# Projections of a transformer block in fp32 parts: the first slice of Wc loaded ahead of x, the first block's transposes in four banks, products begun tile by tile, the other blocks' transposes in two halves

## The chip, the cores and the metric

The kernel runs on one core of one Trainium2 chip, as one program written instruction by instruction for each engine: TensorE (matmuls, transposes), VectorE, ScalarE, GpSimd, and SyncE, which issues most of the loads and stores. The metric is the device time of an execution in microseconds, from which less is better. An engine works its own queue in order; engines wait for one another by semaphores that count up.

## The reference

The kernel computes one transformer layer with conditioning (adaptive layer norm) on x of 2 x 2048 x 512 in float32, with H = 512, 16 heads of 32 and an inner width of 2048:

```python
c6 = jax.nn.silu(c) @ Wc + bc
sh_msa, sc_msa, g_msa, sh_mlp, sc_mlp, g_mlp = jnp.split(c6, 6, axis=-1)
xm = _modulate(_ln(x), sh_msa, sc_msa)          # ln(x) * (1 + scale) + shift
q, k, v = xm @ Wq + bq, xm @ Wk + bk, xm @ Wv + bv
w = softmax((q / DH) k^T) per head
x = x + g_msa * ((w v) @ Wo + bo)
xm2 = _modulate(_ln(x), sh_mlp, sc_mlp)
x = x + g_mlp * (gelu(xm2 @ W1 + b1) @ W2 + b2)
```

c is the condition, 2 x 512; Wc is 512 x 3072, so that c6 has six slices of 512 for each of the two batches.

## The kernel before

The program has three stages one behind the other: `project` (0 to some 350 us of the profile), `attend`, and `feed_forward`. The diff touches only `project`.

**Tiling.** The 4096 tokens are 8 blocks of 512 (`NBLK`, index k, blocks 0 to 3 are batch 0). A block is normalised (`norm`, VectorE; its square root is `root` on GpSimd), transposed by TensorE in four tiles t of 128 features (`transposes`, L604, four 128x128 transposes a tile), scaled and shifted by ScalarE from PSUM into xm (`modulate`, L529, two buffers), and split by VectorE into a high part, rounded to the fp32r format, and a low part, the rest (`split_xm`: the cast L411 and the subtraction L413). Each product is the sum of three matmuls per tile, high by high, high by low, low by high (`three`, L610 to L612), twelve in all. A block has 12 products of this kind (`PER_BLOCK`): m = 0 to 7 are q and k in turn for the four groups of heads, m = 8 to 11 are v for four groups of tokens. They go round four PSUM banks (`mm_bank`). ScalarE takes each result (`take_qk`, L540, L543; L557 for v), VectorE splits those of q and k (`split_qk`, L420, L422), SyncE stores them.

**Order in a block.** The norm of block k + 1 stands at the start of VectorE's part of block k. TensorE transposes block k + 1 after product 3 of block k, ScalarE modulates after taking product 3, VectorE splits xm after splitting product 3. The transposes use two banks (`t_bank`) in turn, and so tile t waits until tile t - 2 has been modulated (the semaphore t_taken, which starts at 2).

**Early maxima.** From block 4 on, TensorE also runs score matmuls for the attention's row maxima (`early`, L644), two behind each of products 4 to 11 (in block 7 other counts), into `c_bank` and `g_bank` in turn. VectorE reduces each (L483). Matmul n waits until the reduce of n - 2 is done, as it uses the same bank. On VectorE the reduces for product m - 1 stand ahead of the `split_qk` of product m (`behind`).

**Start.** SyncE issues six small loads of biases and the condition, then x of block 0 (L273), two slices of Wc (L275), the weights Wq, Wk, Wv and x of block 1, each of 1 MB. TensorE forms silu(c) @ Wc for a slice (`part_rows`, L581), ScalarE copies it (`take_rows`, L522), TensorE turns it to columns (`part_columns`, L590), VectorE adds the bias and, for a scale, 1.0 (`mod_columns`, L441, L445). The first two slices (shift and scale of the attention) are needed for the first `modulate`; the second `part_columns` waits for the first `mod_columns` (g_taken). VectorE's queue there is norm(0), mod_columns(0), high_w(0), mod_columns(1), split_xm(0), and then high and low parts of Wk and Wv. The low part of Wq is GpSimd's (L364). TensorE waits for all four tiles of xm to be split, `pe.wait_ge(xm_split, 2 + KT * (k + 1))`, ahead of the first product of a block, and in each product for its weight's low part, `pe.wait_ge(w_split[m % 2 if m < N_QK else 2], 1)`.

Of the kernel before, what the change touches and what calls it, by code (L numbers as in the profile page):

```python
# [4 lines left out]
F32 = mybir.dt.float32  # L5
# [6 lines left out]
P = 128  # L12
# [162 lines left out]
def project(nc, sh, late, x, c, Wc, bc, Wq, bq, Wk, bk, Wv, bv, b1, bo, b2):  # L175
# [5 lines left out]
    with ExitStack() as ctx:  # L181
# [40 lines left out]

        rows_in, w_in, wide_in = sem("rows_in"), [sem(f"w_in{n}") for n in range(3)], sem("wide_in")
# [8 lines left out]
        w_hi_ready, w_split = sem("w_hi_ready"), [sem(f"w_split{n}") for n in range(3)]  # L232
# [13 lines left out]
        PARTS = (0, 1, 3, 4, 2, 5)  # L246
        RESULTS = (0, 1, 2, 3, 4, 6, 8)
# [4 lines left out]
        LAST_RESULT = 8  # L252

# [15 lines left out]
        def _(sp):  # L269
# [3 lines left out]
            sp.dma_start(xb[0][:, :, :], x_blocks[0]).then_inc(x_in[0], 16)  # L273
# [3 lines left out]
            load_wc(0)  # L277
            load_wc(1)
# [99 lines left out]
        def _(v):  # L378
# [27 lines left out]
            def split_xm(k, q):  # L406

                v.wait_ge(mm_done, PER_BLOCK * (k - 1) + 1) if not isinstance(k, int) or k > 1 else None
                for t in range(KT):
# [18 lines left out]
            v.tensor_scalar(sh.bq_scaled[:, :], sh.vecs[:, ROW_BQ:ROW_BQ + KT], 1.0 / DH, None, ALU.mult).then_inc(vecs_ready, 1)  # L428
            v.wait_ge(const_ready, 5)
# [6 lines left out]
            def mod_columns(e, column, one):  # L436
# [6 lines left out]
                if one:  # L443
                    after(last)
                    last = v.tensor_scalar(sh.mod[:, :, column:column + KT], sh.mod[:, :, column:column + KT], 1.0, None, ALU.add)  # L445
# [10 lines left out]
            def result(e, b):  # L456
                if e == 2:
                    mod_columns(e, SHIFT_MLP, False)
                elif e == 3:
                    mod_columns(e, SCALE_MLP, True)  # L460
                else:
                    gate(e, b)
# [5 lines left out]
            mod_columns(0, SHIFT_MSA, False)  # L468
            high_w(0).then_inc(w_hi_ready, 1)
            mod_columns(1, SCALE_MSA, True)  # L470
            split_xm(0, 0)
            for n in (1, 2):
                after(high_w(n))
                v.tensor_tensor(w_lo[:, n, :, :], w_raw[n], w_hi[:, n, :, :].bitcast(F32), ALU.subtract).then_inc(w_split[n], 1)
# [20 lines left out]
            def body(k, i, q, has_next):  # L495
                if has_next:
                    norm(k + 1, i + q, 1 - q)
                for m in range(N_QK // 2):
                    behind(k, m)
                if has_next:  # L500
                    split_xm(k + 1, 1 - q)
                for m in range(N_QK // 2, N_QK):
                    behind(k, m)
# [1232 lines left out]
```

## Time and profile before

| | |
|---|---|
| time of the kernel, median of 3 runs | 2750.54 us (2748.51 to 2750.82) |
| profiled execution, in all | 2751.63 us |
| its span, from first to last instruction | 2749.8 us |
| mean granted clock of TensorE | 0.995 |

The span is made of busy and idle time on five engines. For each instruction the timeline gives its start and duration; idle time ahead of it is written in brackets with what ended it (the releaser). "PEld" is TensorE loading weights, beside its matmuls. An engine's idle time costs nothing where another engine sets the pace. A matmul's duration contains its way through the array, which overlaps with the next: the distance between two starts is what it costs.

### The profile page before, as it was taken

What the parts mean: (1) busy time and instruction counts of PE and PEld (TensorE: products, weight loads), DVE (VectorE), ACT (ScalarE), POOL (GpSimd) and SP (SyncE); (2) the same over time, 40 slices, a digit from 0 to 9 for tenths busy, and PEclk for the clock granted to TensorE, in tenths of its full rate; (3) what the DMA queues carried; (4) which work ended last, traced back from release to release, by engine and by line L of the source; (5) the groups of instructions that cost most, each with busy time, mean ns of one, the idle gap of its engine ahead of it and who ended that gap; (6) DMA issues with size and microseconds to landing.
All of it is one profiled execution on the core that took longest, in us unless ns stands there. A gap on an engine that the chain in (4) does not pass through costs nothing. (4 is left out here: it accounts for less than half of the span.)

```text
span 2749.8 us, 37932 instructions
## 1 busy us (share of the span) xinstructions
PE 2702.7 (98%) x13737; PEld 1781.6 (65%) x13737; DVE 1999.2 (73%) x3323; ACT 1345.7 (49%) x2537; POOL 1867.9 (68%) x1080
## 2 busy tenths in 40 slices
PE   7999999999999999999999999999999999999998
PEld 5777755555555555555555555554688888888887
DVE  6456688788888888888888888776576765765754
ACT  2322266676676667767676776675221221221211
POOL 1000078989989999999989989896555555455553
PEclk9999999999999999999999999999999999999999
DMA  6555458788888879878888887875400100110000
GB/s 241 186 178 188 157 122 177 166 185 181 176 182 175 187 166 191 182 166 186 172 186 184 173 187 167 194 145 123 146 35 16 47 31 16 46 43 4 31 16 16
DMA packets 143754, 369.22 MB, mean 134 GB/s; under 512 B 23572, under 2 KB 40528, under 8 KB 119760
## 3 DMA queue, kind: packets, MB, share of 16 engines
q0 software_dynamic: 26784, 195.05, 35.5%
q1 hardware_dynamic: 96000, 155.26, 18.9%
q10 hardware_dynamic: 20784, 16.49, 2.0%
q8 instruction: 110, 1.80, 0.3%
q14 instruction: 76, 0.62, 0.1%
HBM read 111.97 MB, written 58.97 MB: 62 GB/s over the span
## 5 line engine op out<-in xcount | busy, mean ns | idle before, releaser
L1059 DVE TENSOR_REDUCE part_max<-shared_bank 128x1 f32<-128x512 f32 x1972 | 1206.8, 679 | 275.3 <-PE shared_bank L1179 275.3
L1034 ACT ACTIVATE probs<-s_bank 128x512 f32<-128x512 f32 x2048 | 1037.1, 629 | 291.7 <-PE s_bank L1195 287.6
L1206 PE MATMUL y_bank<-probs,vs 128*32 128x512 f32 x4096 | 496.2, 602 | 0.0
L881 POOL TENSOR_TENSOR first_sum<-probs 128x1024 f32<-128x1024 f32 x124 | 348.2, 2818 | 79.1 <-ACT probs L1034 77.0
L1622 ACT ACTIVATE h<-shared_bank,vecs 128x512 f32<-128x512 f32 x128 | 88.0, 687 | 564.0 <-PE shared_bank L1646 559.2
L1195 PE MATMUL s_bank<-late_parts 97*128 97x512 f32 x848 | 349.5, 414 | 1.0 <-ACT probs L1034 1.0
L881 POOL TENSOR_TENSOR half_sum<-probs 128x1024 f32<-128x1024 f32 x124 | 340.1, 2775 | 15.2 <-ACT probs L1034 14.9
L892 POOL TENSOR_TENSOR wo<-probs 128x1024 f32<-128x1024 f32 x124 | 338.5, 3115 | 0.4 <-ACT probs L1034 0.4
L1179 PE MATMUL shared_bank<-late_parts 96*128 96x512 f32 x848 | 336.8, 398 | 0.9
L892 POOL TENSOR_TENSOR second_sum<-probs 128x1024 f32<-128x1024 f32 x128 | 320.9, 2670 | 19.4 <-ACT probs L1034 10.2
L1432 POOL TENSOR_TENSOR late_parts<-w_raw,late_parts 128x512 fp32r<-128x512 f32 x96 | 129.1, 1345 | 227.7 <-DVE late_parts L1509 227.7
L1206 PEld LDWEIGHTS y_bank<-probs,vs 128*32 128x32 f32 x4096 | 107.2, 109 | 243.6 <-issue 125.0
L1195 PEld LDWEIGHTS s_bank<-late_parts 97*128 97x128 f32 x848 | 160.1, 189 | 133.4 <-issue 88.0
L1519 DVE CAST h_hi<-h 128x512 fp32r<-128x512 f32 x128 | 79.3, 619 | 179.9 <-ACT h L1622 179.8
L1644 PE MATMUL acc_bank<-w_hi,h_hi 128*128 128x512 f32 x512 | 201.5, 394 | 1.4 <-DVE h_lo L1521 1.2
L1644 PE MATMUL shared_bank<-late_parts 128*128 128x512 f32 x508 | 201.3, 396 | 1.1 <-PEq L740 1.1
L1646 PE MATMUL acc_bank<-w_hi,h_lo 128*128 128x512 f32 x512 | 200.8, 392 | 0.0
L1646 PE MATMUL shared_bank<-late_parts 128*128 128x512 f32 x508 | 199.4, 392 | 0.0
L1645 PE MATMUL acc_bank<-w_lo,h_hi 128*128 128x512 f32 x512 | 199.0, 389 | 0.0
L1645 PE MATMUL shared_bank<-space_parts,late_parts 128*128 128x512 f32 x508 | 198.8, 391 | 0.0
L1179 PEld LDWEIGHTS shared_bank<-late_parts 96*128 96x128 f32 x848 | 161.3, 190 | 30.5 <-DVE part_max L1059 5.4
L1195 PE MATMUL s_bank<-space_parts,late_parts 97*128 97x512 f32 x432 | 177.8, 412 | 0.0
(204 smaller groups left out, 4579.9 us busy)
## 6 DMA issues: line engine op xcount, KB each, us to landing
half_sum<-second_sum POOLq DMA_DIRECT2D x62, 1024.0 KB, 13.5
first_sum<-wo POOLq DMA_DIRECT2D x62, 1024.0 KB, 9.9
half_sum<-first_sum POOLq DMA_DIRECT2D x62, 1024.0 KB, 7.7
q_parts<-qk_out SPq DMA_DIRECT2D x32, 512.0 KB, 3.5
k_parts<-qk_out SPq DMA_DIRECT2D x32, 512.0 KB, 3.5
late_parts<-q_parts SPq DMA_DIRECT2D x63, 256.0 KB, 11.5
late_parts<-k_parts SPq DMA_DIRECT2D x60, 256.0 KB, 11.9
late_plain<-in_x SPq DMA_DIRECT2D x12, 1024.0 KB, 7.5
```

The costliest lines, as they stand in the source:

```text
L881: pool.tensor_tensor(first_home(c)[:, hs, :], probs[:, 4 * c % RING, hs, :], probs[:, (4 * c + 1) % RING, hs, :], ALU.add).then_inc(first_ ...
L892: pool.tensor_tensor(second_home(c)[:, hs, :], probs[:, (4 * c + 2) % RING, hs, :], probs[:, (4 * c + 3) % RING, hs, :], ALU.add).then_inc ...
L1034: act.activation(probs[:, tile % RING, h, :], s_bank[(HPG * tile + h) % 3][:, :], ACT.Exp).then_inc(p_done, 1)
L1059: v.tensor_reduce(part_max[:, i % 2, hs, c:c + 1], m_bank[ring.bank["max", i, n]][:, :], AX.X, ALU.max).then_inc(m_taken, 1)
L1179: pe.matmul(m_bank[ring.bank["max", i, n]][:, :], queries[i % 3][0:STACK, h, s * P:(s + 1) * P], keys[u][0:STACK, h, :], start=True, stop= ...
L1195: pe.matmul(s_bank[n % 3][:, :], keys[u][0:STACK + 1, h, s * P:(s + 1) * P], queries[i % 3][0:STACK + 1, h, :], start=True, stop=True).the ...
L1206: last = pe.matmul(y_bank[h * DH:(h + 1) * DH, :], vs[:, t, h * DH:(h + 1) * DH], probs[:, tile % RING, h, :], start=(t == 0), stop=(t == ...
L1432: pool.tensor_tensor(feed.w1_lo(j), w1_raw[j * 4 // MT][:, :, j % (MT // 4) * P:(j % (MT // 4) + 1) * P], feed.w1_hi(j).bitcast(F32), ALU. ...
L1622: act.activation(h[:, j % 2, :], up_bank[j % 2][:, :], ACT.Gelu, bias=sh.vecs[:, ROW_B1 + j:ROW_B1 + j + 1]).then_inc(up_taken, 1)
L1644: pe.matmul(bank, hi_l, hi_r, start=first, stop=False)
L1645: pe.matmul(bank, hi_l, lo_r, start=False, stop=False)
L1646: return pe.matmul(bank, lo_l, hi_r, start=False, stop=last)
```

## The change

- SyncE issues Wc's first slice ahead of x of block 0.
- The 1.0 of the two scales is added once to the bias columns in `vecs`, at the start, and no longer in `mod_columns`.
- Block 0's transposes of tiles 2 and 3 go to `mm_bank[2]` and `mm_bank[3]` (`x_bank`), so that they wait for no `modulate`.
- The first product of each block waits for xm tile by tile, inside `three`, in place of the wait for all four ahead of it.
- The high part of Wk is made by ScalarE (after its modulate of block 0), and VectorE's subtraction for Wk waits for it (wk_hi_ready).
- For blocks 1 to 7 transposes, modulate and split of xm are done in two halves (`HALF_AT`): tiles 0 and 1 behind product 3 as before, tiles 2 and 3 behind product 4, on each of the three engines.

```diff
--- before.py
+++ after.py
@@ -220,6 +220,9 @@
         g_bank = pb("g_bank", [P, H])
         m_bank = [c_bank, g_bank]
 
+        def x_bank(k, t):
+            return mm_bank[t] if k == 0 and t >= 2 else t_bank[t % 2]
+
         rows_in, w_in, wide_in = sem("rows_in"), [sem(f"w_in{n}") for n in range(3)], sem("wide_in")
         wc_in = [sem(f"wc_in{n}") for n in range(6)]
         x_in = [sem(f"x_in{n}") for n in range(2)]
@@ -229,7 +232,7 @@
         em_done, em_taken, early_neg = sem("em_done"), sem("em_taken"), sem("early_neg")
         silu_ready, select_ready = sem("silu_ready"), sem("select_ready")
         c_done, c_taken, g_done, g_taken = sem("c_done"), sem("c_taken"), sem("g_done"), sem("g_taken")
-        w_hi_ready, w_split = sem("w_hi_ready"), [sem(f"w_split{n}") for n in range(3)]
+        w_hi_ready, wk_hi_ready, w_split = sem("w_hi_ready"), sem("wk_hi_ready"), [sem(f"w_split{n}") for n in range(3)]
         stats_ready, rstd_ready, xn_ready = sem("stats_ready"), sem("rstd_ready"), sem("xn_ready")
         t_done, t_taken, xm_split = sem("t_done"), sem("t_taken"), sem("xm_split")
         mm_done, mm_taken, qk_split = sem("mm_done"), sem("mm_taken"), sem("qk_split")
@@ -244,12 +247,16 @@
         PER_BLOCK = 2 * G + TT
         N_QK = 2 * G
         PARTS = (0, 1, 3, 4, 2, 5)
+        SCALE_PARTS = (1, 4)
         RESULTS = (0, 1, 2, 3, 4, 6, 8)
 
 
         ROWS_AT = {(1, 0): 2, (1, 4): 3, (2, 0): 4, (3, 0): 5}
         RESULT_AT = {(1, 2): (2, 0), (1, 6): (3, 0), (2, 2): (4, 0), (2, 5): (4, 1), (3, 2): (5, 0), (3, 5): (5, 1)}
         LAST_RESULT = 8
+
+
+        HALF_AT = {N_QK // 2 - 1: (0, 1), N_QK // 2: (2, 3)}
 
 
 
@@ -270,11 +277,12 @@
             for r, v, n in ((ROW_BC, bc, 6 * KT), (ROW_BQ, bq, KT), (ROW_BK, bk, KT), (ROW_BV, bv, KT), (ROW_B1, b1, MT)):
                 sp.dma_start(rows[r:r + n, :], v.rearrange("(r p) -> r p", p=P)).then_inc(rows_in, 16)
             sp.dma_start(rows[ROW_C:ROWS, :], c.rearrange("b (t p) -> (b t) p", p=P)).then_inc(rows_in, 16)
-            sp.dma_start(xb[0][:, :, :], x_blocks[0]).then_inc(x_in[0], 16)
+
             def load_wc(e):
                 sp.dma_start(wc[e % 2][:, :, :], wc_parts[PARTS[e]]).then_inc(wc_in[e], 16)
 
             load_wc(0)
+            sp.dma_start(xb[0][:, :, :], x_blocks[0]).then_inc(x_in[0], 16)
             load_wc(1)
             for n, w in enumerate((Wq, Wk, Wv)):
                 sp.dma_start(w_raw[n], w.rearrange("(t p) n -> p t n", p=P)).then_inc(w_in[n], 16)
@@ -403,10 +411,11 @@
                                            ALU.subtract, ALU.mult)
                 last.then_inc(xn_ready, 1)
 
-            def split_xm(k, q):
-
-                v.wait_ge(mm_done, PER_BLOCK * (k - 1) + 1) if not isinstance(k, int) or k > 1 else None
-                for t in range(KT):
+            def split_xm(k, q, ts):
+
+                if k > 1:
+                    v.wait_ge(mm_done, PER_BLOCK * (k - 1) + 1)
+                for t in ts:
                     v.wait_ge(t_taken, 2 + KT * k + t + 1)
                     v.tensor_copy(xm_hi[q][:, t, :], xm[:, t % 2, :]).then_inc(hi_step, 1)
                     v.wait_ge(hi_step, KT * k + t + 1)
@@ -426,6 +435,10 @@
             v.wait_ge(rows_t, 1)
             after(v.tensor_copy(sh.vecs[:, :], c_bank[:, 0:ROWS]))
             v.tensor_scalar(sh.bq_scaled[:, :], sh.vecs[:, ROW_BQ:ROW_BQ + KT], 1.0 / DH, None, ALU.mult).then_inc(vecs_ready, 1)
+            for part in SCALE_PARTS:
+                columns = sh.vecs[:, ROW_BC + part * KT:ROW_BC + (part + 1) * KT]
+                last = v.tensor_scalar(columns, columns, 1.0, None, ALU.add)
+            after(last)
             v.wait_ge(const_ready, 5)
             after(v.tensor_reduce(select[:, :], sh.ident[:, :].rearrange("p (s r) -> p r s", s=KT)[:, 0:B, :], AX.X, ALU.add))
             for b in range(B):
@@ -433,16 +446,13 @@
             last.then_inc(select_ready, 1)
             norm(0, 0, 0)
 
-            def mod_columns(e, column, one):
+            def mod_columns(e, column):
 
                 v.wait_ge(g_done, RESULTS[e] + 1)
                 part = PARTS[e]
                 for b in range(B):
                     last = v.tensor_tensor(sh.mod[:, b, column:column + KT], g_bank[:, :].rearrange("p (t b) -> p b t", t=H // 2)[:, b, 0:KT],
                                            sh.vecs[:, ROW_BC + part * KT:ROW_BC + (part + 1) * KT], ALU.add)
-                if one:
-                    after(last)
-                    last = v.tensor_scalar(sh.mod[:, :, column:column + KT], sh.mod[:, :, column:column + KT], 1.0, None, ALU.add)
                 last.then_inc(g_taken, 1)
 
             def gate(e, b):
...
@@ -465,13 +475,15 @@
                 v.wait_ge(w_in[n], 16)
                 return v.tensor_copy(w_hi[:, n, :, :], w_raw[n])
 
-            mod_columns(0, SHIFT_MSA, False)
+            mod_columns(0, SHIFT_MSA)
             high_w(0).then_inc(w_hi_ready, 1)
-            mod_columns(1, SCALE_MSA, True)
-            split_xm(0, 0)
-            for n in (1, 2):
-                after(high_w(n))
-                v.tensor_tensor(w_lo[:, n, :, :], w_raw[n], w_hi[:, n, :, :].bitcast(F32), ALU.subtract).then_inc(w_split[n], 1)
+            mod_columns(1, SCALE_MSA)
+            split_xm(0, 0, range(KT))
+            v.wait_ge(w_in[1], 16)
+            v.wait_ge(wk_hi_ready, 1)
+            v.tensor_tensor(w_lo[:, 1, :, :], w_raw[1], w_hi[:, 1, :, :].bitcast(F32), ALU.subtract).then_inc(w_split[1], 1)
+            after(high_w(2))
+            v.tensor_tensor(w_lo[:, 2, :, :], w_raw[2], w_hi[:, 2, :, :].bitcast(F32), ALU.subtract).then_inc(w_split[2], 1)
 
             def early(n):
                 v.wait_ge(em_done, n + 1)
@@ -495,12 +507,10 @@
             def body(k, i, q, has_next):
                 if has_next:
                     norm(k + 1, i + q, 1 - q)
-                for m in range(N_QK // 2):
+                for m in range(N_QK):
                     behind(k, m)
-                if has_next:
-                    split_xm(k + 1, 1 - q)
-                for m in range(N_QK // 2, N_QK):
-                    behind(k, m)
+                    if has_next and m in HALF_AT:
+                        split_xm(k + 1, 1 - q, HALF_AT[m])
                 for m in range(N_QK - 1, PER_BLOCK):
                     for n in early_at.get((k, m), ()):
                         early(n)
@@ -521,12 +531,12 @@
                     act.wait_ge(g_done, RESULTS[e - 1])
                 act.activation(c_part[:, e % 2, :], c_bank[:, :], ACT.Copy).then_inc(c_taken, 1)
 
-            def modulate(k, b, t0=0):
-
-                for t in range(KT):
+            def modulate(k, b, ts):
+
+                for t in ts:
                     act.wait_ge(t_done, KT * k + t + 1)
                     act.wait_ge(xm_split, KT * k + t + 1)
-                    act.activation(xm[:, t % 2, :], t_bank[t % 2][:, :], ACT.Identity,
+                    act.activation(xm[:, t % 2, :], x_bank(k, t)[:, :], ACT.Identity,
                                    scale=sh.mod[:, bass.ds(b, 1), SCALE_MSA + t].rearrange("p a -> p (a)"),
                                    bias=sh.mod[:, bass.ds(b, 1), SHIFT_MSA + t].rearrange("p a -> p (a)")).then_inc(t_taken, 1)
 
@@ -549,8 +559,8 @@
                     take_qk(k, (m,))
                     if (k, m) in ROWS_AT:
                         take_rows(ROWS_AT[k, m])
-                    if has_next and m == N_QK // 2 - 1:
-                        modulate(k + 1, next_b)
+                    if has_next and m in HALF_AT:
+                        modulate(k + 1, next_b, HALF_AT[m])
                 for t in range(TT):
                     act.wait_ge(mm_done, 1 + PER_BLOCK * k + N_QK + t + 1)
                     act.wait_ge(v_stored[t % 2], 16 * (k * TT // 2 + t // 2) + 1)
@@ -559,7 +569,9 @@
             take_rows(0)
             take_rows(1)
             act.wait_ge(g_taken, 2)
-            modulate(0, 0)
+            modulate(0, 0, range(KT))
+            act.wait_ge(w_in[1], 16)
+            act.activation(w_hi[:, 1, :, :], w_raw[1], ACT.Copy).then_inc(wk_hi_ready, 1)
             for i in range(0, NBLK // 2 - 1):
                 for q in range(2):
                     body(2 * i + q, (2 * i + q + 1) // BPB, True)
@@ -596,17 +608,20 @@
                 pe.wait_ge(g_taken, RESULTS[e] + b)
                 pe.matmul(g_bank[:, :], select_wide[:, b, :], c_part[:, e % 2, :], start=True, stop=True).then_inc(g_done, 1)
 
-            def transposes(k, q):
+            def transposes(k, q, ts):
                 pe.wait_ge(xn_ready, k + 1)
+                for t in ts:
+                    if k:
+                        pe.wait_ge(t_taken, KT * k + t + 1)
+                    for s in range(TT):
+                        last = pe.transpose(x_bank(k, t)[:, s * P:(s + 1) * P], xb[q][:, s, t * P:(t + 1) * P], sh.ident[:, :])
+                    last.then_inc(t_done, 1)
+
+            def three(bank, hi_l, lo_l, hi_r, lo_r, first_of=None):
+
                 for t in range(KT):
-                    pe.wait_ge(t_taken, KT * k + t + 1)
-                    for s in range(TT):
-                        last = pe.transpose(t_bank[t % 2][:, s * P:(s + 1) * P], xb[q][:, s, t * P:(t + 1) * P], sh.ident[:, :])
-                    last.then_inc(t_done, 1)
-
-            def three(bank, hi_l, lo_l, hi_r, lo_r):
-
-                for t in range(KT):
+                    if first_of is not None:
+                        pe.wait_ge(xm_split, 2 + KT * first_of + t + 1)
                     pe.matmul(bank, hi_l(t), hi_r(t), start=(t == 0), stop=False)
                     pe.matmul(bank, hi_l(t), lo_r(t), start=False, stop=False)
                     last = pe.matmul(bank, lo_l(t), hi_r(t), start=False, stop=(t == KT - 1))
@@ -620,7 +635,7 @@
                     if m < N_QK:
                         n, g = m % 2, m // 2
                         three(bank, lambda t: w_hi[:, n, t, g * P:(g + 1) * P], lambda t: w_lo[:, n, t, g * P:(g + 1) * P],
-                              lambda t: xm_hi[q][:, t, :], lambda t: xm_lo[:, q, t, :])
+                              lambda t: xm_hi[q][:, t, :], lambda t: xm_lo[:, q, t, :], k if m == 0 else None)
                     else:
                         s = m - N_QK
                         three(bank, lambda t: xm_hi[q][:, t, s * P:(s + 1) * P], lambda t: xm_lo[:, q, t, s * P:(s + 1) * P],
@@ -645,11 +660,10 @@
                           start=True, stop=True).then_inc(em_done, 1)
 
             def body(k, q, has_next):
-                pe.wait_ge(xm_split, 2 + KT * (k + 1))
                 for m in range(PER_BLOCK):
                     products(k, q, (m,))
-                    if has_next and m == N_QK // 2 - 1:
-                        transposes(k + 1, 1 - q)
+                    if has_next and m in HALF_AT:
+                        transposes(k + 1, 1 - q, HALF_AT[m])
                     if (k, m) in ROWS_AT:
                         part_rows(ROWS_AT[k, m])
                     if (k, m) in RESULT_AT:
@@ -664,7 +678,7 @@
             part_columns(0)
             part_rows(1)
             part_columns(1)
-            transposes(0, 0)
+            transposes(0, 0, range(KT))
             for k in range(NBLK):
                 body(k, k % 2, k < NBLK - 1)
 
```

## Rows read from the trace of the kernel before

**Rows 1.** The page: span, and part 1, busy us (share) xinstructions

```profile
span 2749.8 us, 37932 instructions
...
PE 2702.7 (98%) x13737; PEld 1781.6 (65%) x13737; DVE 1999.2 (73%) x3323; ACT 1345.7 (49%) x2537; POOL 1867.9 (68%) x1080
```

**Rows 2.** Groups of instructions, 0 to 346 us: busy, mean ns | idle before, releaser

```profile
L604 PE MATMUL t_bank<-ident,late_plain 128*128 128x128 f32 x128 | 20.3, 298 | 6.2 <-ACT xm L529 6.1
```

**Rows 3.** Timeline, 0 to 62 us: start, us, engine, line [idle before <-releaser]

```profile
8.80 2.47 DVE L391 BATCH_NORM_STATS2 stats<-late_plain 128x6 f32<-128x512 f32 x4 [3.33 <-DMA late_plain<-in_x]
...
11.62 1.94 PE L581 MATMUL c_bank<-late_plain,c_silu 128*32 128x512 f32 x8 [7.20 <-DMA late_plain<-in_L_cond_Wc]
...
13.15 1.92 DVE L402 TENSOR_SCALAR late_plain<-late_plain,mv,rstd 128x512 f32<-128x512 f32 x4 [1.15 <-POOL rstd L360]
...
16.93 1.23 DVE L466 CAST w_hi<-space_plain 128x2048 fp32r<-128x2048 f32 x1 [0.47 <-DMA space_plain<-in_L_cond_Wq]
...
18.23 4.52 POOL L364 TENSOR_TENSOR w_lo<-space_plain,w_hi 128x2048 fp32r<-128x2048 f32 x1 [5.12 <-DVE w_hi L466]
...
18.77 1.87 PE L590 MATMUL g_bank<-select,c_part 128*128 128x2 f32 x8 [0.72 <-ACT c_part L522]
...
20.94 1.84 DVE L445 TENSOR_SCALAR mod<-mod 128x8 f32<-128x8 f32 x1
...
23.63 0.43 DVE L411 CAST late_parts<-xm 128x512 fp32r<-128x512 f32 x1 [0.84 <-ACT xm L529]
...
28.03 0.79 PE L610 MATMUL mm_bank<-late_parts,w_hi 128*128 128x512 f32 x1 [2.41 <-DVE xm_lo L413]
...
29.14 2.29 DVE L474 TENSOR_TENSOR w_lo<-space_plain,w_hi 128x2048 fp32r<-128x2048 f32 x1
...
33.74 0.59 PE L611 MATMUL mm_bank<-xm_lo,w_hi 128*128 128x512 f32 x1
...
34.17 0.40 PE L612 MATMUL mm_bank<-late_parts,w_lo 128*128 128x512 f32 x1
```

**Rows 4.** Timeline around the boundary inside block 0, 39 to 49 us

```profile
39.14 1.92 DVE L402 TENSOR_SCALAR late_plain<-late_plain,mv,rstd 128x512 f32<-128x512 f32 x4 [1.13 <-POOL rstd L360]
...
44.69 1.32 PE L604 MATMUL t_bank<-ident,late_plain 128*128 128x128 f32 x8 [1.50 <-ACT xm L529]
45.77 0.48 PE L610 MATMUL mm_bank<-late_parts,w_hi 128*128 128x512 f32 x1
...
48.66 0.40 PE L610 MATMUL mm_bank<-late_parts,w_hi 128*128 128x512 f32 x1
```

**Rows 5.** Timeline around the boundary inside block 1, 81 to 86 us

```profile
81.52 1.03 PE L604 MATMUL t_bank<-ident,late_plain 128*128 128x128 f32 x8
...
83.13 1.33 PE L604 MATMUL t_bank<-ident,late_plain 128*128 128x128 f32 x8 [0.57 <-ACT xm L529]
...
84.53 0.39 PE L611 MATMUL mm_bank<-xm_lo,w_hi 128*128 128x512 f32 x1
```

**Rows 6.** Timeline of the feed-forward stage, 2300 to 2312 us

```profile
2300.12 1.29 POOL L1432 TENSOR_TENSOR late_parts<-w_raw,late_parts 128x512 fp32r<-128x512 f32 x1 [5.35 <-DVE late_parts L1509]
...
2300.65 1.04 DVE L1514 CAST w_hi<-w_raw 128x512 fp32r<-128x512 f32 x1 [0.61 <-PE acc_bank L1646]
```

**Rows 7.** Groups of ScalarE, shapes apart: busy us, mean ns of one

```profile
L1617 ACT ACTIVATE late_parts<-late_plain 128x512 fp32r<-128x512 f32 x28 | 15.3, 619 | 0.0
```

**Rows 8.** Timeline of block 5, 243 to 248 us, and of block 7, 344 us

```profile
243.99 0.39 PE L644 MATMUL c_bank<-space_parts 96*128 96x512 f32 x1
...
244.91 0.43 DVE L420 CAST qk_out<-qk 128x512 fp32r<-128x512 f32 x1
...
245.98 0.68 DVE L483 TENSOR_REDUCE part_max<-c_bank 128x1 f32<-128x512 f32 x1
...
247.26 0.39 PE L644 MATMUL c_bank<-space_parts 96*128 96x512 f32 x1
...
343.70 0.50 PE L644 MATMUL c_bank<-space_parts,late_parts 96*128 96x512 f32 x1 [0.56 <-DVE part_max L483]
```

More of the change, by code:

```diff
@@ L457, in result @@
                 if e == 2:
-                    mod_columns(e, SHIFT_MLP, False)
+                    mod_columns(e, SHIFT_MLP)
                 elif e == 3:
-                    mod_columns(e, SCALE_MLP, True)
+                    mod_columns(e, SCALE_MLP)
                 else:
```

## Prediction

> **What bounds the kernel now.** The page first: one core, and TensorE is busy for 98% of the span [rows 1]. What TensorE waits for or does again is therefore worth its own length wherever it is taken away. The grouped instructions of the projection stage (0 to 346 us, the only stage that the diff touches) give two losses: 6.2 us of idle time before transposes (L604), nearly all until ScalarE's xm, over eight blocks [rows 2]; and the start, where the first product issues at 28.03 [rows 3]. The timeline splits the first: at the boundary inside block 0 TensorE waits 1.50 us [rows 4]; inside block 1 it waits 0.57, and again before tile 3 [rows 5]; the boundaries inside blocks 2 to 6 have the same 0.57 (this row stands for six). Behind the projections every stage is ordered behind them by TensorE, so I carry what they gain to the end one for one.
>
> **Part 1: the start.** Four things change: the order of x and Wc's first slice, the +1.0 in the scale columns, Wk's high part on ScalarE, and the order of transposes and products.
>
> Before, x is in at 8.80 and Wc's first slice at 11.62 [rows 3]. Both are 1 MB on one queue, so I swap these times: Wc at 8.8, x at 11.6. The norm of block 0 runs from 8.80 to 13.15 + 1.92 = 15.07, 6.27 long; it now ends at 11.6 + 6.27 = 17.9. Wc is used earlier, but VectorE's queue is strict: mod_columns(0) stands behind norm(0), so the second part_columns, 1.87 long (it waits for g_taken), starts at about 18.1 in place of 18.77, and the transposes of block 0 follow it 0.6 earlier than before. Also behind norm stands high_w(0): 16.93 before, now 17.9 + 0.2 = 18.1. GpSimd's w_lo for Wq, 4.52 long and 1.30 behind that cast's start, so moves from 18.23..22.75 to about 19.4..23.9.
>
> What does VectorE do meanwhile? The removed +1.0 op shows it: 8 elements took 1.84 us, from 20.94 to 22.78, and GpSimd's op ended at 22.75 [rows 3]. It waited for GpSimd. The add is now made at 5 us into idle engines, and mod is ready at about 20.4 in place of 22.78; the first cast followed 0.85 later (23.63), and so could come before 22. But the first cast of split_xm is of the same kind. In the feed-forward stage a cast issued while GpSimd ran took 1.04 us, and ended 0.28 behind GpSimd's end (2301.41) [rows 6]; alone it takes 0.43 [rows 3]. The Trainium skill ("SBUF — State Buffer", "Who interferes with whom") has the rule behind it: VectorE's copies and casts in the fast mode and GpSimd take turns at a shared port pair for whole instructions; the trace agrees in both rows. It speaks against this change, because x second makes the w_lo later; without it the sum below would be about 1.9 larger.
>
> So the first cast ends at 23.9 + 0.3 = 24.2 (before 24.06), its subtraction at 24.9. A tile of split costs VectorE 1.07 us ((28.03 - 23.63 - 0.14) / 4, the 0.14 being the end of the pipe and the semaphore). Before, TensorE waited for all four; now for one: products start at 24.9, 3.1 us earlier. At the low rate (0.43 us from the matmul at 33.74 to that at 34.17, 512 columns at 1.2 GHz [rows 3]) three matmuls take 1.28 a tile, more than 1.07, so it never waits for tiles 1 to 3. Product 0 ends at 24.9 + 12 x 0.43 = 30.1.
>
> Product 1 needs Wk's low part. Before: 29.14 + 2.29 = 31.43, when product 0 was still running [rows 3]. Now the split ends at 23.75 + 4 x 1.07 = 28.0; ScalarE's last modulate starts when tile 1 is split (25.9) and ends some 0.9 later (a plain copy of that size takes 0.619 [rows 7]), at 26.8; then comes its copy of 128x2048. No ScalarE row has that size: at least VectorE's cast of it, 1.23 [rows 3], at most four of ScalarE's 0.619 [rows 7], 2.48. I take 1.9, since part of the 0.619 is paid once an instruction. Then 28.7 + 2.3 = 31.0 (30.3 to 31.6). TensorE waits about 0.9 us there, a new wait; the 3.1 is down to what this chain allows. VectorE's chain behind it (Wv's parts, norm(1)) is unchanged and ended at 39.14 + 1.92 = 41.06 [rows 4]; it now ends at 40.6. Products 1 to 3 take 36 x 0.235 = 8.5 at the high rate (45.77 to 48.66 is product 4 of block 0, twelve matmuls and 0.06 for the switch from transposes [rows 4]) and end at 39.5: TensorE waits for xn_ready, until 40.7.
>
> **Part 2: halves.** From rows 5: the transposes of block 1 begin at 81.52 and the second product matmul behind them at 84.53, so the effective start of product 4 is 84.53 - 0.235 = 84.30: 2.78 us. Without waits, eight transposes take 0.87 (1.03 less the 0.27 of one's tail, over seven steps, is 0.109 each); I add 0.06 per switch. Two halves: 1.86. The half behind product 4 hides ScalarE's work: the wait for the first modulated tile ended at 83.13 [rows 5], and t_bank is wanted again only at 81.52 + 0.93 + 2.8 = 85.3. Gain 0.9 a block. The waits by tile in the first product of each block were fulfilled long before; I cost them at nothing (0.1 a block at most).
>
> Block 0: with the halves, product 5 starts at 40.7 + 1.86 + 2.82 = 45.4, against 48.66 before [rows 4]: 3.3 us. From 1.2 (clock late, below) to 3.9; with the copy at its upper bound 2.7. I take 3.0. Blocks 1, 2 and 3: 3 x 0.9 = 2.7.
>
> Blocks 4, 5 and 6 also issue two early maxima behind each of products 4 to 11, and VectorE's order matters. Call E the end of product 4 (243.99 in block 5). Before, the split of all tiles was done when VectorE came to product 4; its split_qk started at E + 0.92 (244.91) and took 1.07, and the first reduce ran at 245.98 [rows 8]. Now tiles 2 and 3 are split between the two: the first reduce runs at E + 1.99 + 2.13 = E + 4.12, 0.68 long, the second ends at about E + 5.45. TensorE: transposes 0.93, then two maxima and product 5, together 247.26 - 243.99 = 3.27, so it comes to the next two maxima at E + 4.2, and each waits for the reduce that frees its bank; the second starts at E + 5.45 where E + 4.43 was due (half the 0.47 that two take, 3.27 less 12 x 0.235, behind the first): 1.0 us lost. That TensorE does stop there is seen at 343.70, 0.56 us until part_max [rows 8]. In the following periods VectorE has 1.07 + 2 x 0.68 = 2.4 us of work per 3.27 and catches up. So 0.9 - 1.0 = -0.1 a block, -0.3 in all. Bounds: from +2.7 (no stop) to -2.
>
> **Sum.** 3.0 + 2.7 - 0.3 = 5.4 us. The profiled execution took 2751.6 in all, 1.8 of it outside its span of 2749.8 [rows 1]; it lies 1.1 above the median 2750.5, inside the scatter of the runs. I set the sum against the median: 2745.1.
>
> **Rivals.**
> B, the early maxima never stop TensorE (VectorE gets its tiles sooner than I think): 5.4 + 3.0 = 8.4, 2742.1. For it: only 1.0 us decides. Against: VectorE's order is fixed.
> C, the clock comes late. The high rate came at 34.17, 6.1 us behind the first product, TensorE busy throughout [rows 3]. By that the new start would have it at 31.1 and lose nothing; but the 0.9 us wait at 30.1 lies right before, and if it puts the rise off to 37 or so, 6 us at low rate cost 2.7, of which 1.2 are hidden by the wait for xn_ready: gain 3.5 to 3.9, 2746.8. The Trainium skill ("TensorE: Matmul & The Clock Gate", "What's actually happening") says that the moment of the rise varies from run to run, since the monitor does not start with the kernel; no run here shows it yet, and by it C happens in some executions and not in others.
> D, the start gives nothing: x or Wk's part is later than I have it by the 3 us won. Then 5.4 - 3.0 = 2.4, 2748.1.
> E, slower: the stop at the early maxima does not pass but returns behind every product from 5 to 11, 7 x 1.0 x 3 blocks = 21 us against gains of 8.4: 2763. It decides if VectorE's work per period passes TensorE's 3.3 us. Against: it is 2.4, which leaves 0.9 us of every period.
>
> **How the numbers follow.** The sum as computed 0.55, B 0.17, C 0.15, D 0.08, E 0.05. 0.2% is 5.5 us, about what a measurement of this kernel can tell from no change, and my sum lies on it: half of the first case and B are faster by over it, 0.44; slower E, 0.05; within it 0.51. The range takes in B to D, less the outer edge of D: 2741.8 to 2748.0, which leaves out E and half of D.
>
> **What would show it.** First product near 24.9 and the first cast of split_xm ending just behind GpSimd's w_lo; a wait of TensorE of some 0.9 us at 30 for w_lo and one for xn_ready at 40; no wait before L604 in blocks 1 to 3 and product 5 there 0.9 us sooner after product 3; two waits of L644 before part_max, about 1.0 in sum, once each in blocks 4, 5 and 6. Wrong it would be by a first cast that runs beside w_lo, a clock that rises before 28 or after 36, or no wait of L644.

## The result, and the profile after

The changed kernel takes 2740.75 us (median of 7 runs, 2739.01 to 2744.91), the kernel before 2750.45 on the same count (2748.11 to 2751.22): 9.7 us less. The ratio is 0.9972 with a 95% interval of 0.9962 to 0.9981, that is 5.2 to 10.5 us, and 7.7 at its middle. I forecast 2745.1 with a range down to 2741.8, and gave "faster by over 0.2%" 0.44 and "within" 0.51. Most steps were right; the gain was larger than the sum. The interval reaches from just under 0.2% to 0.38%: with its middle at 0.28% "faster", to which I gave the smaller chance, is the likelier of the two, and "within" is only just not excluded. The median lies 1.05 us below the range; 7.7 us less than 2750.45 would be 2742.7, inside it. When the kernel before was timed again (23 runs and then 9), its medians were 2748.23 and 2749.73, so a part of the 9.7 us may be that its seven runs came out long.

The page after:

```profile
span 2738.6 us, 37946 instructions
...
PE 2699.0 (99%) x13737; PEld 1780.1 (65%) x13737; DVE 1996.4 (73%) x3322; ACT 1345.6 (49%) x2538; POOL 1868.1 (68%) x1080
```

Against [rows 1] the span is 11.2 us shorter and TensorE 3.7 us less busy: most of what went is idle time. The group of the transposes (now L617), 0 to 346 us; the eight of block 0 that go to `mm_bank` are a group of their own, without idle time:

```profile
L617 PE MATMUL t_bank<-ident,late_plain 128*128 128x128 f32 x120 | 16.6, 284 | 0.9 <-DVE late_plain L410 0.9
```

The 6.2 us of idle time of [rows 2] are 0.9, and they are no longer a wait for ScalarE but for the norm of block 1, in block 0.

The start on the timeline, to be laid beside [rows 3]:

```profile
8.37 1.94 PE L593 MATMUL c_bank<-late_plain,c_silu 128*32 128x512 f32 x8 [3.85 <-DMA late_plain<-in_L_cond_Wc]
...
10.95 2.47 DVE L399 BATCH_NORM_STATS2 stats<-late_plain 128x6 f32<-128x512 f32 x4 [5.12 <-DMA late_plain<-in_x]
...
17.28 1.22 DVE L476 CAST w_hi<-space_plain 128x2048 fp32r<-128x2048 f32 x1
...
18.57 4.53 POOL L372 TENSOR_TENSOR w_lo<-space_plain,w_hi 128x2048 fp32r<-128x2048 f32 x1 [3.30 <-DVE w_hi L476]
...
19.38 0.23 DVE L454 TENSOR_TENSOR mod<-g_bank,vecs 128x4 f32<-128x4 f32 x2 [0.89 <-PE g_bank L602]
...
21.20 2.19 DVE L420 CAST late_parts<-xm 128x512 fp32r<-128x512 f32 x1 [1.58 <-ACT xm L539]
...
24.27 0.77 PE L625 MATMUL mm_bank<-late_parts,w_hi 128*128 128x512 f32 x1 [1.41 <-DVE xm_lo L422]
```

Wc's slice is in at 8.37 and x at 10.95. GpSimd's w_lo runs from 18.57 to 23.10, and the first cast of split_xm, issued at 21.20, takes 2.19 us and ends at 23.39, 0.29 behind it. The first product follows at 24.27 (forecast 24.9). Then, beside [rows 4]:

```profile
25.96 1.90 ACT L574 ACTIVATE w_hi<-space_plain 128x2048 fp32r<-128x2048 f32 x1
...
27.97 2.29 DVE L484 TENSOR_TENSOR w_lo<-space_plain,w_hi 128x2048 fp32r<-128x2048 f32 x1 [0.66 <-ACT w_hi L574]
...
30.41 0.47 PE L625 MATMUL mm_bank<-late_parts,w_hi 128*128 128x512 f32 x1 [1.60 <-DVE w_lo L484]
...
37.96 1.92 DVE L410 TENSOR_SCALAR late_plain<-late_plain,mv,rstd 128x512 f32<-128x512 f32 x4 [1.13 <-POOL rstd L368]
...
39.94 1.09 PE L617 MATMUL t_bank<-ident,late_plain 128*128 128x128 f32 x8 [0.85 <-DVE late_plain L410]
...
43.66 1.18 PE L617 MATMUL t_bank<-ident,late_plain 128*128 128x128 f32 x8
...
44.59 0.48 PE L625 MATMUL mm_bank<-late_parts,w_hi 128*128 128x512 f32 x1
```

ScalarE's copy of 128x2048 took 1.90, as estimated. TensorE waits 1.60 us for Wk's low part (forecast 0.9), and 0.85 for xn_ready. Product 4 of block 0 runs between the two sets of transposes (40.8 to 43.7), so the matmul at 44.59 is product 5's first: 4.1 us earlier than 48.66. In block 1 ([rows 5]) the first set begins at 77.50, 4.0 us sooner than the 81.52 of before, the second behind product 4 at 81.16, and neither waits:

```profile
77.50 1.04 PE L617 MATMUL t_bank<-ident,late_plain 128*128 128x128 f32 x8
...
81.16 1.03 PE L617 MATMUL t_bank<-ident,late_plain 128*128 128x128 f32 x8
```

Block 4, where the early maxima begin (now L659):

```profile
194.86 1.04 PE L617 MATMUL t_bank<-ident,late_plain 128*128 128x128 f32 x8
...
195.65 0.47 PE L659 MATMUL c_bank<-space_parts 96*128 96x512 f32 x1
...
196.85 0.42 DVE L420 CAST late_parts<-xm 128x512 fp32r<-128x512 f32 x1
...
198.98 0.68 DVE L495 TENSOR_REDUCE part_max<-c_bank 128x1 f32<-128x512 f32 x1
...
199.58 0.68 DVE L495 TENSOR_REDUCE part_max<-g_bank 128x1 f32<-128x512 f32 x1
...
199.72 0.50 PE L659 MATMUL c_bank<-space_parts 96*128 96x512 f32 x1 [0.56 <-DVE part_max L495]
...
200.32 0.50 PE L659 MATMUL g_bank<-space_parts 96*128 96x512 f32 x1
```

VectorE splits tile 2 from 196.85 on and tile 3 behind it, then come the two reduces; TensorE, there for the next maximum, waits 0.56 us for part_max at 199.72, and starts the one behind it only at 200.32, when the second reduce is done (199.58 + 0.68). The same pair in [rows 8] (block 5, 247.26) had no wait. The forecast stop is there, in each of blocks 4, 5 and 6.

ScalarE's takes of v give a mark that every trace has. The row has their number, the shortest, median and longest in ns, and the starts of the first and the last; the last stands at the end of the projections:

```profile
L567 ACT ACTIVATE v_out<-mm_bank x32: 597/599/601, 56.1 to 340.4; 128x512 f32<-128x512 f32 x32
```

Before it was 347.0. So the profiled projections are 6.6 us shorter; my sum was 5.4. By the last take of v of each block: 4.0 us by the end of block 0, then 5.1 and 6.1 by the ends of blocks 1 and 2, 7.2 by the first take of block 3, 7.0, 6.8 and 6.6 by the ends of blocks 4 to 6, and 6.6 at the end. The other 4.6 us of the 11.2 come behind the projections, where nothing was changed.

### The profile page after: what moved, and what is told of

Read it like the earlier page. It is cut to its first block and busy times, and to the rows that moved or that the text cites. A ratio compares the mean times of both kernels' runs of the same rounds, so it can differ in the third digit from the quotient of the medians.

```text
span 2738.6 us, 37946 instructions
## 1 busy us (share of the span) xinstructions
PE 2699.0 (99%) x13737; PEld 1780.1 (65%) x13737; DVE 1996.4 (73%) x3322; ACT 1345.6 (49%) x2538; POOL 1868.1 (68%) x1080
## 5 line engine op out<-in xcount | busy, mean ns | idle before, releaser
L895 POOL TENSOR_TENSOR first_sum<-probs 128x1024 f32<-128x1024 f32 x124 | 339.3, 2736 | 81.7 <-ACT probs L1048 79.5
## 6 DMA issues: line engine op xcount, KB each, us to landing
late_parts<-q_parts SPq DMA_DIRECT2D x63, 256.0 KB, 11.6
```

The lines of the kernel that those rows point to most:

```text
L895: pool.tensor_tensor(first_home(c)[:, hs, :], probs[:, 4 * c % RING, hs, :], probs[:, (4 * c + 1) % RING, hs, :], ALU.add).then_inc(first_ ...
```

## The experiments

All traces have two marks: the last take of v, and the last take of y (in the attention). The table gives them for every kernel; times with an interval are there where a kernel was also timed.

| kernel | last take of v | last of y less last of v | time |
|---|---|---|---|
| before, three traces | 347.0, 348.4, 348.5 | 1594.2, 1588.2, 1594.5 | ratio 1 |
| changed, three traces | 340.4, 340.2, 340.5 | 1590.6, 1592.2, 1588.7 | 0.9972 (0.9962 to 0.9981) |
| start alone | 347.4 | 1593.8 | 1.0007 (0.9998 to 1.0016) |
| halves alone | 341.4 | 1591.2 | 0.9972 (0.9963 to 0.9981) |
| x first | 339.9 | 1588.8 | 0.9972 (0.9961 to 0.9983) |
| reduces first | 337.5 | 1586.8 | 0.9959 (0.9946 to 0.9971) |
| Wq on VectorE | 339.2 | 1589.0 | one run, 2738.20 |
| all tiles awaited | 340.3 | 1593.6 | one run, 2743.02 |
| Wk on VectorE | 341.6 | 1590.4 | one run, 2741.10 |
| reduces first and Wq on VectorE | 336.2 | 1590.3 | 0.9952 (0.9939 to 0.9966) |

**The start alone.**

```diff
-        HALF_AT = {N_QK // 2 - 1: (0, 1), N_QK // 2: (2, 3)}
+        HALF_AT = {N_QK // 2 - 1: (0, 1, 2, 3)}
```

> The changed kernel with all its edits at the start, but transposes, modulate and split of a block's xm together behind product 3, as before. Theory (both parts need each other in block 0): TensorE reaches block 0's boundary at 39.9, but the third tile's bank is free only when ScalarE has modulated tile 0, which stands behind its take of product 3 at about 42.7; product 5 of block 0 starts at about 47.5 against 48.66 before and 44.6 + 2.8 = 47.4 less one half of transposes in the changed kernel. Worth about 1.2 us of the projections' 6.6, and each later boundary idles 0.57 us again. Rival (the start is worth by itself what my sum gave it): 3 to 4 us.

Nothing that can be measured is won (0.9998 to 1.0016). The timeline at block 0's boundary shows where the start's gain goes:

```profile
40.29 1.03 PE L617 MATMUL t_bank<-ident,late_plain 128*128 128x128 f32 x8
...
43.50 1.79 PE L617 MATMUL t_bank<-ident,late_plain 128*128 128x128 f32 x8 [2.18 <-ACT xm L539]
```

In the first trace of before the first set begins here:

```profile
42.15 1.04 PE L604 MATMUL t_bank<-ident,late_plain 128*128 128x128 f32 x8
```

TensorE is at the boundary 1.9 us sooner than that (40.29 against 42.15), but its second set starts only 1.2 us sooner (43.50 against 44.69): tile 2's bank is free when ScalarE has modulated tile 0, behind a take that waits for VectorE, and the idle time grows from 1.50 to 2.18. The view of stretches (busy time and count of each engine, then the granted clock, the DMA share and GB/s) adds:

```profile
30.10:33.50 3.40, 3.11 (x7) 2.48 (x8) 3.37 (x3) 0.00 (x0) 0.00 (x0) 0.50 0.53 194
33.50:43.70 10.20, 8.02 (x40) 6.41 (x39) 8.75 (x22) 2.99 (x5) 1.01 (x1) 1.00 0.15 54
43.70:47.10 3.40, 3.40 (x13) 2.88 (x12) 3.30 (x7) 1.96 (x3) 0.00 (x0) 0.50 1.01 381
```

In 43.7 to 47.1 the granted clock is half, 1.2 GHz, behind that wait, and so it is from 30.1, in the last 0.3 us of the one for Wk's low part (2.08 us in this trace). That takes the 1.2 us back: the last take of v of block 0 is at 68.61, against 68.44 in the first trace of before, where the clock did not fall. In the second and third traces of before (below) it falls at the same place, and there block 0 ends at 69.86 and 69.89: against those the start alone is 1.3 us sooner, as estimated, and 1.0 to 1.1 at the end (347.4 to 348.4 and 348.5). So in the traces the 1.2 us are there at like clock; in the timed runs they aren't seen. The rival's 3 to 4 is out.

**The halves alone.** The start as before: L273 ahead of the first slice of Wc, two banks with the wait for t_taken, the 1.0 in mod_columns, all four tiles awaited, Wk's high part on VectorE. The core of the edit against the changed kernel:

```diff
-                    if first_of is not None:
-                        pe.wait_ge(xm_split, 2 + KT * first_of + t + 1)
+                    if first_of is not None and t == 0:
+                        pe.wait_ge(xm_split, 2 + KT * first_of + KT)
...
-            act.activation(w_hi[:, 1, :, :], w_raw[1], ACT.Copy).then_inc(wk_hi_ready, 1)
```

> The kernel before with the halves alone: x first, the 1.0 added in mod_columns, two transpose banks, all tiles of xm awaited, Wk's high part on VectorE. Theory: about 1.8 us in block 0, 1.05 in each of blocks 1, 2 and 3, and a loss of about 0.2 in each of blocks 4, 5 and 6: 4.4 us of the projections' 6.6. Rival (parts add up: 4.0 for the start and the rest for halves): 2.6 us.

5.6 us less than the first trace of before, 6.6 less than the mean of three: nearly all of the change, and more than the 4.4 of the theory. Blocks 1 to 3 gave 1.0 to 1.1 each, 4 to 6 lost 0.2 each, as expected; the difference is block 0, 3.0 (68.44 to 65.47) in place of 1.8. In this trace the high clock came at 31.5, in the first trace of before at 34.2; 2.7 us at half the clock are 1.35 us of work, an estimate that covers it. In the kernel before an earlier rise was spent in the longer wait at the boundary (second and third traces, below), and with halves there is no such wait. The start adds 1.0 (341.4 to 340.4) in one trace each; the timed ratios are both 0.9972.

**x first.**

```diff
+            sp.dma_start(xb[0][:, :, :], x_blocks[0]).then_inc(x_in[0], 16)
             load_wc(0)
-            sp.dma_start(xb[0][:, :, :], x_blocks[0]).then_inc(x_in[0], 16)
```

> The changed kernel with x of block 0 loaded ahead of Wc's first slice again. Theory: the order is worth nothing or costs a little, since norm(0) then ends some 2.5 us sooner, Wq's high part is cast as soon as it is loaded, and GpSimd's w_lo, for which the first cast of split_xm waits, ends 0.3 us sooner or more: first product 0.3 to 1 us sooner, projections shorter by as much. Rival (Wc's path to the scale and shift is the longest, which is why it was moved ahead): first product about 1 us later.

```profile
17.96 4.52 POOL L371 TENSOR_TENSOR w_lo<-space_plain,w_hi 128x2048 fp32r<-128x2048 f32 x1 [5.12 <-DVE w_hi L475]
...
22.21 0.55 DVE L419 CAST late_parts<-xm 128x512 fp32r<-128x512 f32 x1 [1.59 <-ACT xm L538]
...
23.64 0.76 PE L624 MATMUL mm_bank<-late_parts,w_hi 128*128 128x512 f32 x1
```

The theory held: w_lo starts 0.6 us sooner, the first product comes at 23.64 in place of 24.27, and the projections end 0.5 sooner. The new order of the loads costs half a microsecond in the traces, since what all wait for is GpSimd's w_lo, and that stands behind the norm; the timed ratio, 0.9972 in both, doesn't resolve it.

**Reduces first.**

```diff
                 for m in range(N_QK):
                     behind(k, m)
+                    if has_next and m == N_QK // 2:
+                        for n in early_at.get((k, m), ()):
+                            early(n)
                     if has_next and m in HALF_AT:
                         split_xm(k + 1, 1 - q, HALF_AT[m])
```

(and `behind(k, 5)` no longer makes them in these blocks)

> The changed kernel, in which VectorE in blocks 4 to 6 makes the two reduces of the early maxima behind product 4 ahead of the second half of split_xm. Theory: TensorE's two waits for part_max in each of these blocks go, 1.0 us a block, projections 3.0 us shorter than in the changed kernel, median about 2737.8. Rival (the waits only move, to the next pair of maxima or to ScalarE's takes): less than 1 us.

```profile
196.37 0.69 DVE L431 TENSOR_TENSOR qk_out<-qk,qk_out 128x512 fp32r<-128x512 f32 x1
...
196.98 0.68 DVE L495 TENSOR_REDUCE part_max<-c_bank 128x1 f32<-128x512 f32 x1
...
197.58 0.68 DVE L495 TENSOR_REDUCE part_max<-g_bank 128x1 f32<-128x512 f32 x1
...
198.18 0.42 DVE L420 CAST late_parts<-xm 128x512 fp32r<-128x512 f32 x1
...
199.13 0.39 PE L663 MATMUL c_bank<-space_parts 96*128 96x512 f32 x1
```

The reduces now run at 196.98 and 197.58, and the next maximum (199.13) does not wait. The last take of v is 2.9 us sooner, 340.4 to 337.5: the stop costs what the sum gave it, and does not move elsewhere. The median of the timed runs is 2734.74 (forecast 2737.8), but the interval of the ratio still overlaps that of the changed kernel; it is the trace that shows the 2.9.

**Wq's low part on VectorE.**

```diff
-            high_w(0).then_inc(w_hi_ready, 1)
+            after(high_w(0))
+            v.tensor_tensor(w_lo[:, 0, :, :], w_raw[0], w_hi[:, 0, :, :].bitcast(F32), ALU.subtract).then_inc(w_split[0], 1)
```

(and GpSimd's is taken out)

> The changed kernel with Wq's low part made by VectorE (2.3 us, right behind its high part) instead of GpSimd (4.5 us). Theory (the first cast of split_xm waits for GpSimd's whole instruction): the cast starts at about 21.9 and takes 0.42, not 2.19; first product at about 23.1 in place of 24.27, and Wk's low part, norm(1) and the end of the projections about 1.1 us sooner (339.3 on the timeline's last take of v, 340.4 in the changed kernel). Rival (the long cast has another cause, or VectorE's extra 2.3 us delays the scale by as much): first product not sooner, projections the same or longer.

```profile
18.38 2.29 DVE L478 TENSOR_TENSOR w_lo<-space_plain,w_hi 128x2048 fp32r<-128x2048 f32 x1
...
21.66 0.43 DVE L418 CAST late_parts<-xm 128x512 fp32r<-128x512 f32 x1 [0.85 <-ACT xm L538]
...
22.96 0.77 PE L624 MATMUL mm_bank<-late_parts,w_hi 128*128 128x512 f32 x1 [0.25 <-DVE xm_lo L420]
```

With GpSimd idle the same cast takes 0.43. The rival was right that the scale comes later (20.59 against 19.38), but less is lost by that than the cast gives back. First product at 22.96, projections 1.2 us shorter.

**All tiles awaited.** The first hunk of the diff shown for the halves alone, made in the changed kernel.

> The changed kernel in which TensorE waits for all four tiles of xm ahead of a block's first product again. Theory (behind the first product stands the wait for Wk's low part at 30.3, then that for xn_ready at 39.9, and they absorb most of it): first product at 27.4, 3.1 us later, but its end at 30 to 32.5 by the clock, and block 0 ends 0 to 2.5 us later, about 1 us. Rival (the 3.1 us go through): 3 us.

```profile
27.27 0.77 PE L625 MATMUL mm_bank<-late_parts,w_hi 128*128 128x512 f32 x1 [4.57 <-DVE xm_lo L422]
...
34.58 0.69 ACT L553 ACTIVATE qk<-mm_bank,vecs 128x512 f32<-128x512 f32 x1 [2.13 <-PE mm_bank L627]
...
37.78 1.92 DVE L410 TENSOR_SCALAR late_plain<-late_plain,mv,rstd 128x512 f32<-128x512 f32 x4 [1.13 <-POOL rstd L368]
...
40.03 1.03 PE L617 MATMUL t_bank<-ident,late_plain 128*128 128x128 f32 x8
```

The first product comes 3.0 us later than at 24.27, and block 0 ends where it did (340.3 against 340.4 at the end). TensorE reaches the boundary at 40.03, 0.33 us after the norm of block 1 is done (37.78 + 1.92), so it doesn't wait there. Products begun tile by tile gain next to nothing here, 0.3 us at most: the 3 us are spent in the waits for Wk's low part and for xn_ready.

**Wk's high part on VectorE.**

```diff
-            v.wait_ge(w_in[1], 16)
-            v.wait_ge(wk_hi_ready, 1)
+            after(high_w(1))
```

(and ScalarE's copy is taken out)

> The changed kernel in which VectorE makes Wk's high part itself again, behind split_xm. Theory: Wk's low part ends at 27.3 + 1.2 + 2.3 = 30.9 instead of 30.26, product 1 and xn_ready(1) come 0.6 us later, and so does the end of the projections. Rival (the wait is hidden): no difference; or 1.2 us, the length of the cast, if ScalarE's copy were free.

```profile
32.58 0.63 PE L623 MATMUL mm_bank<-xm_lo,w_hi 128*128 128x512 f32 x1
...
38.82 1.91 DVE L410 TENSOR_SCALAR late_plain<-late_plain,mv,rstd 128x512 f32<-128x512 f32 x4 [1.13 <-POOL rstd L368]
...
41.32 1.03 PE L614 MATMUL t_bank<-ident,late_plain 128*128 128x128 f32 x8
```

The projections end 1.2 us later (341.6), but not all of that is the edit. 0.3 is a later load in this trace (its first product starts at 24.61 against 24.27). The norm of block 1 ends at 40.73 against 39.88, 0.85 later, which less the load is 0.5, near the theory's 0.6. The rest is the clock: it is half from 31.9 to 35.3 (the matmul at 32.58 takes 0.63, not 0.40), and TensorE comes to the boundary only at 41.32, 0.6 us after the norm, without a wait. So the theory's size fits, and the rival's 1.2 is met only by the fall of the clock.

**Both mends.**

> The changed kernel with the reduces of the early maxima ahead of the second half of split_xm and Wq's low part on VectorE, together. Theory: the 2.9 us that the reduces gave and the 1.1 us of the cast add, since one lies in block 0 and the other in blocks 4 to 6: last take of v at 336.4, 4.0 us sooner than in the changed kernel; median about 4 us below it. Rival (the start is absorbed by a later wait): 2.9 us.

They add: 336.2, 4.2 us less than the changed kernel. Its ratio to before, 0.9952, is the best seen, but its interval overlaps that of "reduces first", and just that of the changed kernel.

**Each kernel again.** The same sources, for more traces.

> The changed kernel once more, for a second trace. Theory: projections as in the first trace (last take of v at 340.4, within 0.5), and the length from the 28th to the last take of y in the attention (212.5 us in the first trace) differs by up to 4 us with the number of stretches at TensorE's low clock in it, about 0.6 us for each us at the low clock. Rival (the shorter tail belongs to the change): 212.5 again.

> The changed kernel a third time: projections again at 340.4, and the stretch from the 28th to the last take of y as the low clock falls in it, by the theory; 212.5 by the rival.

> The kernel before once more, for a second trace. Theory: projections as in the first trace (347.0), but the same stretch of the attention, 216.3 us in the first trace, anywhere from 210 to 217 with the number of low-clock stretches. Rival (it belongs to the kernel): 216.3 again.

> The kernel before a third time: projections again at 347.0, and the stretch from the 28th to the last take of y as the low clock falls in it, by the theory; 216.3 by the rival.

The changed kernel's projections repeat within 0.3 us. Those of before don't: twice they end 1.4 us later than in the trace that I predicted from. The third trace of before at block 0's boundary, and its stretches:

```profile
41.07 1.06 PE L604 MATMUL t_bank<-ident,late_plain 128*128 128x128 f32 x8
...
44.60 1.61 PE L604 MATMUL t_bank<-ident,late_plain 128*128 128x128 f32 x8 [2.48 <-ACT xm L529]
```

```profile
41.00:45.40 4.40, 1.91 (x14) 1.41 (x14) 4.26 (x9) 2.71 (x4) 0.00 (x0) 1.00 0.46 174
45.40:48.80 3.40, 3.40 (x11) 2.82 (x12) 3.26 (x8) 1.55 (x2) 0.00 (x0) 0.51 1.02 381
48.80:52.00 3.20, 3.20 (x14) 2.55 (x14) 1.59 (x3) 0.69 (x1) 0.00 (x0) 0.98 0.04 13
```

The high clock had come sooner (31.9 in place of 34.2), TensorE was at the boundary at 41.07 in place of 42.15, idled 2.48 us in place of 1.50, and at 45.4 the granted clock fell to half for 3.4 us. The second trace has the same: a wait of 2.39, and half the clock from 45.7 to 49.1. Mean of before 348.0, of after 340.4: 7.6 us, close to the 7.7 at the middle of the ratio's interval.

The rest varies too. From the 28th to the last take of y (210 us) near the two ends are the third trace of before, 216.5 us, and that of "reduces first", 209.9:

```profile
1726.50:1943.00 216.50, 209.59 (x1119) 107.71 (x1123) 145.45 (x222) 142.84 (x277) 166.32 (x91) 0.95 0.63 141
```

```profile
1714.40:1924.30 209.90, 205.02 (x1119) 105.79 (x1123) 147.08 (x222) 142.78 (x276) 169.09 (x91) 0.98 0.64 145
```

With the mean granted clock at 0.95 two traces of different kernels took 216.5 and 216.7, at 0.98 four took 209.9 to 212.6, with before's second trace at 210.2 among them, and the changed kernel had 215.2 in its second (0.96). The clock isn't all of it: at 0.96 the traces range from 212.7 to 216.3. So the 3.8 us that this stretch gave in the first pair (216.3 to 212.5) are no property of the change.

## Why the prediction was nearly right

- **Block 0, forecast 3.0, measured 4.0 in the first pair and 5.0 against the mean of before's three traces.** The chain was as forecast: cast behind w_lo, Wk's low part, xn_ready. Everything in it was 0.6 to 0.8 us early (the norm of block 1 ends at 39.88, not 40.6), because x was in at 10.95, not 11.6: swapping the landing times was too coarse. The larger miss is in the kernel before: its 1.50 us wait in one trace was the mild case, and in two of three traces the same wait is longer and the clock falls behind it. The sum was made against one execution.
- **Blocks 1 to 3, 2.7 forecast.** Measured 1.0 to 1.1 a block where I had 0.9: the term is mis-sized by 0.15 each. The waits by tile cost nothing: blocks 2 and 3 take as long with them as without.
- **Blocks 4 to 6, -0.3 forecast, -0.6 measured.** The stop at the early maxima was there, 1.0 us a block, and as I had worked it out: from the end of product 4 (194.86 in block 4) the first reduce starts 4.12 us on, forecast 4.12, and the second maximum 5.46, forecast 5.45. "Reduces first" took 2.9 us back. The 0.3 by which the term was off is 0.1 a block, half of it in the halves' gain, which without the stop is 0.85 here. Rival B is out, and E too: the stop comes once a block.
- **Rival C (clock late)** did not come; in the changed kernel the rise was seen at 27.6, about 21.9 and 28.3. Two of these lie before 28, which I had named as a sign of being wrong: product 0 ended 1.4 us sooner than forecast, but the wait for Wk's low part took that up (1.60 in place of 0.9). What came instead was a fall of the clock: in the changed kernel only in the second trace, 25.3 to 28.7 inside product 0, where the wait for Wk's low part hides it; in three of its variants at that wait ("start alone", "reduces first", "Wk on VectorE"), where the wait for xn_ready hides all but 0.35 to 0.55 us. The Trainium skill ("TensorE: Matmul & The Clock Gate", "What's actually happening") has it that the monitor runs freely against the kernel; that the same source shows the rise at three times and the fall in some traces alone agrees with it.
- **Rival D (the start gives nothing)** is the one that I undervalued. Alone the start gives nothing in the timed runs (about 1.2 us in the traces at like clock), on top of the halves 1.0 us, and of its edits the order of loads costs 0.5, the waits by tile give 0.3 at most, and Wk's high part on ScalarE 0.5. The 1.0 in the bias columns and the four banks were not tried apart; by difference most of the start's 1.0 would be theirs. I had costed the start as if block 0's gain belonged to it; most of it is the halves'.
- **Below the range by 1.05 us:** 9.7 less 5.4 is 4.3 us. Of these the terms above give 1.2 (6.6 in the first pair) to 2.2 (7.6 over three traces each). The rest is not explained by the diff: behind the projections the three traces of before scatter by 6.3 us and those of the changed kernel by 3.5, and two medians of seven runs need not wash that out; this last is inferred from the traces, not tried by itself.

What stays open: why the clock falls in one trace and not in another at the same wait, and what the 1.0 in the bias columns and the four banks are worth each.

## What to carry to other kernels

Split a block of work on an engine in two halves with other work between where the engine that empties its buffers is behind: here that was worth 6 us, nearly all of the gain. Then look at what was queued behind it on the third engine: VectorE's reduces, put behind the new half, cost 3 us here, and one change of order gave them back. Starting a consumer sooner is worth nothing if two later waits don't move with it; follow the chain to the last wait before you count the gain, and make the sum against more than one trace.

## What the runs showed of the hardware

Some waits of TensorE in the middle of dense work came with a stretch at half the granted clock, and others of the same length did not. At the boundary of block 0, where only transposes stand beside the wait, it fell after 2.18 us ("start alone", 43.7 to 47.1), 2.39 and 2.48 (second and third traces of before, from 45.7 and 45.4), and not after 1.50 (first trace of before). At the wait for Wk's low part it fell with 2.08 us ("start alone", from 30.1), 2.09 ("reduces first", from 29.9) and 1.87 ("Wk on VectorE", from 31.9), and not with 2.08 ("x first", and both mends), 2.10 ("Wq on VectorE") or 1.60 (first trace of the changed kernel). So the length of the wait alone doesn't decide. The projections of before ended 1.4 us later in the two traces with the fall.

A VectorE cast that was issued while GpSimd ran an op from SBUF to SBUF ended 0.29 us behind it (2.19 us long, 0.43 with GpSimd idle). ScalarE's copy of 128x2048 from SBUF to SBUF took 1.90 us.
